# Projecting two batches ahead inside the attention stages of a two-layer transformer kernel

## The reference

```python
def modulate(x, shift, scale):            # layer norm, then the batch's scale and shift
    ...
# layer 0, attention: 16 heads of 8 channels, one k and one v for all heads
q = (x @ Wq + bq).reshape(Bx, Tx, HEADS, HD); k = x @ Wk + bk; v = x @ Wv + bv
q, k = rope(q), rope(k)
att = softmax(causal(q k^T / sqrt(8)));  out = (att v) @ Wo + bo
# layer 0, feed-forward: the best of 8 experts, at most 640 tokens each
h = relu(tokens_e @ w1[e] + b1[e]);  answer = h @ w2[e] + b2[e]   # 128 -> 512 -> 128
# layer 1, attention: no mask, q and k divided by their length over 128 channels
q, k, v = split(x @ qkv_w^T);  q, k = l2norm(q), l2norm(k)
att = softmax(q k^T / sqrt(8) / temperature);  out = (att v) @ proj_w^T + proj_b
# layer 1, feed-forward: two layers of attention in windows of 64 tokens, with a gated MLP
```

## Time and profile before

| | us |
|---|---|
| median of 3 runs | 2424.55 |
| fastest and slowest of them | 2423.39, 2437.38 |
| the profiled execution, its own time | 2432.8 |
| span of the profile | 2430.8 |
| PE / DVE / ACT / POOL busy | 1873.0 / 1448.5 / 1157.3 / 892.7 |
| PE's weight loads busy | 976.6 |

### The profile page before, as it was taken

The page is one execution under the profiler, slowest core; times in us unless marked ns, Lnnn a source line. Parts: engine busy times, 40 slices in busy tenths (PEclk is TensorE's granted clock), DMA queues, the critical chain, the costliest instruction groups (busy, mean ns, idle before and its releaser), DMA issues. The chain is left out here.

```text
span 2430.8 us, 43279 instructions
## 1 busy us (share of the span) xinstructions
PE 1873.0 (77%) x12804; PEld 976.6 (40%) x12868; DVE 1448.5 (60%) x2514; ACT 1157.3 (48%) x2802; POOL 892.7 (37%) x999
## 2 busy tenths in 40 slices
PE   5528999884618455629999999557999999999996
PEld 3314444432516334422222222234555555555552
DVE  4426767751401233317888888126888888888882
ACT  1115656560003111104667667305777677677672
POOL 3223344341140332310111111116666677666670
PEclk9768889895559765657999989758999999999997
DMA  3432323322013223232333332130111111111110
GB/s 107 133 101 74 112 92 107 108 84 84 14 63 103 83 85 101 72 94 72 99 108 108 104 105 80 65 111 25 31 48 31 33 43 38 39 52 41 38 49 20
DMA packets 137868, 179.90 MB, mean 74 GB/s; under 512 B 14896, under 2 KB 82355, under 8 KB 137520
## 3 DMA queue, kind: packets, MB, share of 16 engines
q1 hardware_dynamic: 135728, 174.59, 23.3%
q0 software_dynamic: 2048, 4.16, 0.6%
HBM read 97.22 MB, written 66.06 MB: 67 GB/s over the span
## 5 line engine op out<-in xcount | busy, mean ns | idle before, releaser
L910 DVE TENSOR_REDUCE M_sb<-banks 128x1 f32<-128x512 f32 (+3 forms) x1024 | 539.8, 581 | 228.0 <-PE banks L727 124.8
L812 ACT ACTIVATE probs_sb<-banks 128x512 f32<-128x512 f32 (+3 forms) x1024 | 473.5, 520 | 254.9 <-PE banks L753 250.8
L724 PE MATMUL banks<-K_sb,Q_sb 72*128 72x512 bf16 (+3 forms) x1024 | 373.8, 371 | 107.8 <-DMA V_sb<-v_dram 71.5
L753 PE MATMUL banks<-Q_sb,K_sb 75*128 75x512 bf16 (+3 forms) x1024 | 358.6, 357 | 5.9 <-ACT probs_sb L812 3.9
L767 PE MATMUL banks<-probs_sb,V_sb 128*32 128x512 f32 (+3 forms) x2048 | 249.9, 556 | 11.8 <-ACT osum_sb L823 8.6
L724 PEld LDWEIGHTS banks<-K_sb,Q_sb 72*128 72x128 bf16 x1024 | 103.2, 101 | 385.2 <-DVE M_sb L910 225.2
L1773 ACT ACTIVATE l_p_sb<-banks,l_nb_sb,l_inv_sb 128x128 f32<-128x128 f32 x512 | 228.0, 465 | 12.7 <-DVE l_nb_sb L1945 12.5
L1851 POOL TENSOR_TENSOR l_inv_sb<-l_clip_sb,l_minus_half_sb 128x16 f32<-128x16 f32 x64 | 186.2, 2909 | 57.2 <-DVE l_clip_sb L1920 55.3
L1859 POOL TENSOR_TENSOR l_pn_sb<-l_p_sb,l_rs_sb 128x512 f32<-128x512 f32 x128 | 150.1, 1173 | 145.5 <-DVE l_rs_sb L1951 144.0
L1844 POOL TENSOR_TENSOR l_ts_sb<-l_t_sb 128x1024 f32<-128x1024 f32 x64 | 153.4, 2396 | 41.1 <-DVE l_t_sb L1899 24.0
L1579 PE MATMUL banks<-lw_sb,l_xs_sb 128*128 128x512 f32 x256 | 127.8, 623 | 26.4 <-DMA l_xs_sb<-hx 22.8
(11 more groups left out here) (205 smaller groups left out, 3575.1 us busy)
## 6 DMA issues: line engine op xcount, KB each, us to landing
Q_sb<-qk_dram SPq DMA_DIRECT2D x192, 96.0 KB
v_dram<-vpad_sb SPq DMA_DIRECT2D x16, 1024.0 KB, 8.5
V_sb<-v_dram SPq DMA_DIRECT2D x64, 256.0 KB
o_dram<-osum_sb SPq DMA_DIRECT2D x64, 256.0 KB, 5.3
l_vs_sb<-l_vt_sb SPq DMA_DIRECT2D x112, 128.0 KB, 2.3
qk_dram<-parts_sb SPq DMA_DIRECT2D x96, 128.0 KB
K_sb<-qk_dram SPq DMA_DIRECT2D x32, 288.0 KB
x_norm_sb<-x SPq DMA_DIRECT2D x24, 256.0 KB, 2.7
```

The costliest lines, as they stand in the source:

```text
L724: mm = pe.matmul(out[:, 0:width], g.Q[0:RK, slot, h, k * P:(k + 1) * P], g.K[0:RK, slot, hk(h), 0:width], start=True, stop=not causal)
L753: pe.matmul(SB[ring % 3][:, t0:N], g.K[0:RM, q, hk(h), k * P:(k + 1) * P], g.Q[0:RM, q, h, t0:N], start=True, stop=True).then_inc(s["b_sco ...
L812: act.activation(g.probs[:, k, h, t0:N], SB[ring % 3][:, t0:N], ACT.Exp, scale=scale)\
L910: dve.reduce_max(g.M[:, u % 2, k, h:h + 1], SA[ring % 3][:, 0:width], AX.X, negate=True)\
```

## The change

`project` becomes `project_first`: it projects the first two batches of a layer only (`FIRST = 2`). Attention batch i then carries the projection of batch i+2 as steps at fixed places between its tiles, on all five engines, and the last two attention batches of a layer carry none. All the new products use bank 7. In layer 0 the A tiles of a unit now run from the widest chunk down. The rest of batch i-1 moves back a little (`normalise`, `out_project`, `residual`, the reciprocals). In the experts, the weights are loaded while routing scatters tokens, tiles are doubled, and PE turns the next expert's tokens between the two products of this one.

Here n is a tile's number in its unit (0 to 15) and (q, n) a place in a batch: unit q, after tile n. Of the edit, cut to what matters (new functions are called from these places):

```diff
+FIRST = 2
-def project(g, layer, x):
+def project_first(g, layer, x):
-    lo, hi = B * layer, B * (layer + 1)
+    lo = B * layer
+    hi = lo + FIRST
...
+    def query_chunk(j):
+        return CH - 1 - j if causal else j
...
-        batch(lo, True, False)
-        with engine.Fori(lo + 1, hi - 1) as i:
-            batch(i, False, False)
-        batch(hi - 1, False, True)
+        batch(lo, True, False, True, True)
+        with engine.Fori(lo + 1, hi - FIRST - 1) as i:
+            batch(i, False, False, True, True)
+        batch(hi - FIRST - 1, False, False, True, False)
+        batch(hi - FIRST, False, False, False, False)
+        batch(hi - 1, False, True, False, False)
```

On SP:

```diff
+                if u == UNITS:
+                    sp.wait_ge(ps["parts_stored"], ahead_of(i, 2 * PARTS * 16, 0))
+                    sp.wait_ge(ps["v_stored"], ahead_of(i, 17, 0))
...
+                    if q == 1 and more:
+                        sp.wait_ge(ns["xc"], normed(i, 1))
+                        load_x(i + 1)
+                    if q == 2 and ahead and causal:
+                        store_parts(i, 0)
                     if q == 3:
                         if not first:
                             store(i)
                         sp.dma_start(g.xres[:, :], x[i - lo]).then_inc(s["x_loaded"], 16)
+                        if ahead:
+                            store_v(i)
+                            if not causal:
+                                store_parts(i, 0)
+                            store_parts(i, 1)
+            def store_v(i):
+                sp.wait_ge(ps["v_stored"], ahead_of(i, 17, 1))
+                sp.dma_start(g.v_dram[i + FIRST].rearrange("c p m -> p c m"),
+                             g.vpad[:, :, :, :].rearrange("p c h w -> p c (h w)")).then_inc(ps["v_stored"], 16)
+            def store_parts(i, w):
+                sp.wait_ge(ps["part3"], ahead_of(i, 2, w + 3))
+                for part in range(PARTS):
+                    sp.dma_start(g.qk_dram[i + FIRST, w, :, part].rearrange("u d h n -> u (d h) n"),
+                                 g.parts[:, w, part, :]).then_inc(ps["parts_stored"], 16)
```

On PE, first the waits ahead of the turned maxima (`turn_max`), then the places of the new products:

```diff
+                if ahead and u == 1:
+                    pe.wait_ge(ns["veps"], normed(i, 1))
+                if ahead and u == 2:
+                    pe.wait_ge(ps["rb"] if causal else f["raw"], ahead_of(i, 2, 1) if causal else i * 4 + (4 - lo * 4))
+                if ahead and u == 3:
+                    pe.wait_ge(ps["rb"] if causal else ps["rot"], ahead_of(i, 2, 2))
+                if ahead and u == 4:
+                    pe.wait_ge(ps["v_stored"], ahead_of(i, 17, 1))
...
+                if (q, n) == (0, 0):
+                    mean(i)
+                if (q, n) == (0, 4):
+                    variance(i)
+                if (q, n) == (0, 12):
+                    spread(i)
+                if (q, n) == (3, 2):
+                    values(i)
+                if causal:
+                    for m, at in enumerate(((1, 0), (1, 4), (1, 11), (2, 0))):
+                        if (q, n) == at:
+                            rotated(i, m)
+                else:
+                    for w, at in enumerate(((1, 0), (1, 4))):
+                        if (q, n) == at:
+                            plain(i, w)
+                    if (q, n) == (1, 10):
+                        norm_sums(i)
+                    for w, at in enumerate(((2, 1), (2, 4))):
+                        if (q, n) == at:
+                            spread_norms(i, w)
...
-                            if (q, k, h) == (2, 0, 2) and not first:
-                                out_project(i, i * 4 + 3)
+                            if (q, k, h) == (2, 2, 3) and not first:
+                                out_project(i, i * 4 + 4)
```

On ACT and then on DVE (POOL has such a list too, by chunks):

```diff
+                if (q, n) == (0, 3):
+                    square(i)
+                if not causal and (q, n) in ((1, 2), (1, 6)):
+                    raw(i, n // 4)
+                for w, at in enumerate(((1, 11), (2, 9)) if causal else ((2, 4), (2, 8))):
+                    if (q, n) == at:
+                        part1(i, w)
+                for w, at in enumerate(((1, 15), (2, 14)) if causal else ((2, 11), (2, 14))):
+                    if (q, n) == at:
+                        part2(i, w)
...
+                if (q, n) == (0, 1):
+                    center(i)
+                if (q, n) == (0, 5):
+                    epsilon(i)
+                if (q, n) == (0, 13):
+                    finish_norm(i)
+                if (q, n) == (3, 3):
+                    copy_v(i)
...
-                            if q == 1 and k < 2 and h % 2 == 1 and not first:
-                                invert_sums(i, 2 * k + h // 2)
+                            if q == 1 and n in (3, 7, 9, 14) and not first:
+                                invert_sums(i, (3, 7, 9, 14).index(n))
```

In the experts, on PE:

```diff
-                    pe.wait_ge(s["biased"], (i * 2 + par + 1) * ST)
+                    widen(e, par, i)
+                    if not (last and par):
+                        turn(e + 1, par ^ 1, i + par)
+                    narrow(e, par)
```

More of the change, by code:

```diff
@@ L214, in paired @@
 def paired(engine, lo, hi, batch):
-    with engine.Fori(0, (hi - lo) // 2 - 1) as j:
-        for slot in range(2):
-            batch(j * 2 + (lo + slot), slot, False)
+    if hi - lo > 2:
+        with engine.Fori(0, (hi - lo) // 2 - 1) as j:
+            for slot in range(2):
+                batch(j * 2 + (lo + slot), slot, False)
     batch(hi - 2, 0, False)
@@ L678, in store, with batch @@
                 sp.dma_start(x_out[i - lo - 1], g.xnew[:, :]).then_inc(s["x_stored"], 16)
-            def batch(i, first, last):
+            def batch(i, first, last, ahead, more):
                 for q in range(UNITS):
@@ L774, in out_project, with mean @@
                 pe.wait_ge(s["mrows"], mrows)
+                pe.wait_ge(s["ytmp"], i - 1)
                 pe.matmul(MB[:, :], g.wo[:, layer, :], g.onorm[:, :], start=True, stop=True).then_inc(s["yacc"], 1)
-            def batch(i, first, last):
+            def mean(i):
+                pe.wait_ge(f["x_loaded"], i * 16 + (16 - FIRST * layer * 16))
+                pe.wait_ge(s["mrows"], i * 4 + 1)
+                if isinstance(i, int) and i == lo:
+                    pe.wait_ge(s["mrows"], i * 4 + 2)
+                pe.matmul(MB[:, :], g.mean_w[:, :], g.xn[:, 0, :], start=True, stop=True).then_inc(ns["mean"], 1)
@@ new lines, in norm_sums @@
+            def norm_sums(i):
+                pe.wait_ge(f["raw"], i * 4 + (4 - lo * 4))
+                pe.wait_ge(s["mrows"], i * 4 + 3)
+                for w in range(2):
+                    for c in range(CH):
+                        at = CH * w + c
+                        mm = pe.matmul(MB[:, at:at + 1], g.ra[:, w, c * P:(c + 1) * P], g.ones_w[:, 0:1],
+                                       start=True, stop=True, skip_group_check=True)
+                mm.then_inc(ps["l2_sums"], 1)
@@ new lines, in widen @@
+            def widen(e, par, nth):
+                pe.wait_ge(g.ewload[par], nth * 64 + 64)
+                pe.wait_ge(s["xT"], e * 2 + 2)
+                for f in range(FT):
+                    for half in range(2):
+                        n = f * 2 + half
+                        if not (isinstance(e, int) and e * 8 + n < 4):
+                            pe.wait_ge(s["relu"], e * 8 + n - 3)
+                        pe.matmul(g.bank[2 + n % 4][:, 0:HALF], g.ew1[:, par, f * P:(f + 1) * P],
+                                  g.exT[:, par, half * HALF:(half + 1) * HALF], start=True, stop=True)\
+                          .then_inc(s["hidden"], 1)
@@ new lines, in narrow @@
+            def narrow(e, par):
+                pe.wait_ge(s["relu"], e * 8 + 8)
+                for t in range(ST):
+                    if not (isinstance(e, int) and e * ST + t < 2):
+                        pe.wait_ge(s["biased"], e * ST + t - 1)
+                    bank = g.bank[6 + (par * ST + t) % 2]
+                    for f in range(FT):
+                        mm = pe.matmul(bank[:, 0:C], g.eh[:, par, f, t * P:(t + 1) * P],
+                                       g.ew2[:, par, f * C:(f + 1) * C], start=(f == 0), stop=(f == FT - 1))
+                    mm.then_inc(s["answer"], 1)
@@ new lines, in two, with _ @@
+            def two(i, first, last):
+                for par in range(2):
+                    e = i * 2 + par
+                    widen(e, par, i)
+                    if not (last and par):
+                        turn(e + 1, par ^ 1, i + par)
+                    narrow(e, par)
+            turn(0, 0, 0)
+            pairs(pe, two)
+        @block.scalar
+        def _(act):
+            def two(i, first, last):
+                for par in range(2):
+                    e = i * 2 + par
+                    if not first:
+                        act.wait_ge(s["answer"], (e - 1) * ST)
+                    for f in range(FT):
@@ L1232, in _ @@
[L1232 to L1242 removed]
```

(12 more changed lines are left out.)

367 lines of the change are left out of this document (274 added, 93 removed).

## The result

The changed kernel takes 2357.47 us (median of 4 runs, 2354.9 to 2366.91), the kernel before 2430.97 in the runs beside it: a ratio of 0.970, interval [0.966, 0.974]. It is faster, as forecast, but by 73 us where the working came to 167, and it lies above the range.

| term | forecast | measured |
|---|---|---|
| first tile of layer 0 earlier | -97.8 | -98.5 |
| attention of layer 0 | +29.6 | +60.3 |
| gate and routing | 0 | -4.7 |
| experts | -20 | -21.3 |
| projection of layer 1 | -143.3 | -146.3 |

A forecast was written before the change was run, and what follows sets the result against it. PE, busy nine tenths of both attentions, was taken as the bound, with projection batches a chain of store latency. Sum: 2432.8 - 241.1 + 29.6 + 64.8 - 20 = 2266.1 us, as a median 2258; range 2200 to 2345.

The forecast's parts named there:

- What the stages lose: Projection stages end with batch 1, so they lose 97.8 us in layer 0 and 143.3 in layer 1.
- the experts: Weights loaded during routing's scatter, next expert's turn between the two products: 20 us gained, of 21 if all is covered.
- the order of the maxima tiles: Layer 0 attention, maxima and score tiles both wide first: between 0 and 4 us a batch gained, 2 taken.
- The first tile of layer 0: Sign to look for: the first attention tile of layer 0 comes near 81 us.
- Stores and loads on one queue: Attention, SP's queue: next unit's loads wait behind v and part stores; 4 us in layer 1, nothing in layer 0.
- three stores leave a unit earlier: Layer 0 attention: three of six part stores go one unit earlier, so no wait for loads was priced there.
- the queue rules: Rival: the full 8.9 us of part stores stand before the next unit's load in both layers; median 2364, chance 0.20.
- What PE's present idle time takes up: Attention: DVE catches up during PE's projection work; credit of 5 us a batch in layer 1, 1.2 in layer 0.
- the hand-overs: Attention: round trips through PSUM bank 7 make PE wait 1.6 us a batch in layer 0, 2.5 in layer 1.

The follow-up runs named there:

- both spread: Changed kernel with loads of q and k at 8 outermost rows for 3 and part stores at 32 for 4, same bytes: 2230.32 us, ratio 0.916.
- the small stores: Changed kernel with each part store in attention writing 64 of 512 columns, the rest filled once in the first stage: 2402.94 us, longer first stages included.
- Either spread alone: Changed kernel with only the loads at 8 outermost rows: 2310.03 us; with only the part stores at 32, k in three loads: 2287.2 us.
- the old kernel spread: Kernel before the change, its loads and part stores given more outermost rows, nothing projected ahead: 2293.26 us, ratio 0.942.

## Why the prediction went wrong

**Held.** What the stages lose (98.5 and 146.3 against 97.8 and 143.3), the experts (21.3 against 20), the order of the maxima tiles (2.9 against 2.0). The first tile of layer 0 came at 79.97 against 81. In layer 0 the sum of the terms other than the stores nearly held: 50.3 to 52.1 us a batch with the stores' bytes gone, forecast 50.0. That both spread gives 50.2 is luck, for spreading takes 4.4 us off the old kernel too: from 40.9 to 50.2 projecting costs 9.3 us there, where 50.0 - 44.4 = 5.6 was forecast.

**Failed: "Stores and loads on one queue".** The steady batches, six of each layer, hold nearly the whole miss: 4.4 and 11.6 us each, 96 of the 99 us. The term was 4 us a batch in layer 1 and nothing in layer 0. By the yardstick of both spread it is 75.6 - 64.1 = 11.5 us and 54.4 - 50.2 = 4.2, which is the upper end, since the old kernel gains by spreading as well. Old and new compared as written and then both spread, the few engines add 22.4 - 13.9 = 8.5 us to what the change costs in layer 1, and 10.0 - 9.3 = 0.7 in layer 0; by the bytes of the small stores it is 4 to 9 and 2 to 4. The parts depend on each other and have no one size; every yardstick is above the forecast.

Two things went wrong in the term. The prediction read the four engines of sixteen from the earlier trace rows, priced the part stores as a length of queue, 8.9 us, and took half of it as past; v, named there, got no price. But v, x and the residual hold every engine first, the part stores move at their lone rate until 1132, 4 us after the loads' issue, and only then do the loads run, themselves at a share of 0.19. Either spread alone leaves 3.0 or 2.4 us of the wait, both together none. And "three stores leave a unit earlier" was taken to be enough in layer 0; the small stores show that their bytes cost 2 to 4 us there. The order on the queue, on which the working spent its care, decides little: stores issued elsewhere or later only moved the wait.

The rule cited from the Trainium skill's "DMA: Bandwidth & Descriptors" ("Rules for kernel authors"), that an outermost dimension of size c below 16 confines the whole DMA to at most c engines, was weighed there and set aside for a middle value. By it the loads with 3 outermost rows run on at most 3 engines: 3/16 = 0.19, the share measured. Taken at its word it gave the case "the queue rules", at 2364 within 7 us of the result, in part by luck: of its two parts the one of layer 0 was too large (58.9 against 54.4) and that of layer 1 a little small (72.9 against 75.6). That the engines are the same ones is argued from the rule; the trace doesn't name them.

**Failed: what a wait costs behind it.** No term of the forecast had the clock. Behind the wait of 7.4 us it is 0.52 for 9.5 us, some 4.6 us of work at full speed. But a stretch at half clock comes in unit 1 without that wait too. PE is busy 64.69 us a batch in the changed kernel, 61.12 with both spread and 48.21 in the old kernel spread: so 3.6 us went with the loads' wait, and another 12.9 - 9.3 = 3.6 of half clock stayed.

**Failed in layer 1: "What PE's present idle time takes up", and the hand-overs with it.** 5.0 us were credited, where PE idles 2.9 us a batch in all. With no load waited for in either kernel, projecting costs 64.1 - 50.2 = 13.9 us: 9.3 of products, 3.6 of half clock and 0.9 of idle time, where 9.3 + 2.5 - 5.0 = 6.8 was forecast. Nothing of the credit is seen in it. What the old kernel had in stock went by spreading alone, 2.5 us of half clock and 0.9 of idle time a batch. The hand-overs had the right size as waits (one of 1.8 us ahead of the turned maxima, which the prediction had named, and 0.3 to 0.7 elsewhere), but not in what stands behind them. That this wait is what lowers the clock in unit 1 is likely from its place and isn't shown: no run took the waits away.

## What to carry to other kernels

Before a transfer is laid beside others, read from a stretch where it runs alone what share of the DMA engines it takes, and the same for those it will meet: here two transfers on three and four of sixteen delayed each other, another queue and another place for the stores didn't help, and another order of their dimensions did. A wait of the matmul engine is to be priced with what stands at half clock behind it, and a short wait too (here 1.8 us, with up to 13 us at half clock behind). And a fix that an experiment finds is to be tried on the old kernel too: here it gave the old kernel some 140 us, and the change 63 on top. Without that run the whole gain of spreading would have been charged to the change.

## What the runs showed of the hardware that was not expected

The time to issue a DMA isn't fixed: six equal part stores took 4.10 us ahead of attention in the old kernel (157.05), 6.81 in a batch of layer 1 of the changed one, and 5.4 there with an eighth of the bytes or both spread; on ACT's queue they went from 0.7 us each to 1.9 and 1.75. What sets it isn't shown, but a slow pattern costs the issuer as well. The spread stores, with 32 outermost rows, reached a share of 0.59 where they ran as they were issued: six in 3.77 us is one of 131 KB every 0.63 us, 209 GB/s, close to the 202 measured. In a batch of the kernel with both spread, where they stand behind v, every engine is busy with them:

```profile
1105.00:1106.00 1.00, 1.00 (x9) 0.16 (x9) 1.00 (x3) 1.00 (x3) 0.00 (x0) 1.00 1.08 375
```

So what held them at 0.59 was the pace of issue.
